# Who stores c and when x is asked for, in the first stage of a two-layer LoRA and FFN kernel

## The reference

```python
def _L0_cond_ref(x, adapter_mapping, W, b, lora_As, lora_Bs):   # x: (128 batches, 32 tokens, 512)
    base_out = einsum('bti,oi->bto', x, W) + b                   # W: 512 x 512
    A  = lora_As[adapter_mapping]                                # per batch: 512 x 16
    Bm = lora_Bs[adapter_mapping]                                # per batch: 16 x 512
    lora_h   = einsum('bti,bir->btr', x, A)
    lora_out = einsum('btr,bro->bto', lora_h, Bm)
    return base_out + lora_out * SCALING
x = x + _L0_ffn_ref(_L0_cond_ref(x, itok_B_0_23, ...), ...)      # silu(c Wg) * (c Wu) Wd, 512 -> 1376 -> 512
x = x + _L1_ffn_ref(_L1_cond_ref(x, itok_B_0_7, ...), ...)       # two layers with routers and experts
```

## Time and profile before

| what | value |
|---|---|
| median of 3 runs | 1004.67 us (1004.18 to 1007.02) |
| profiled execution, its own time | 1005.67 us |
| its span in the trace | 1003.9 us |
| TensorE busy | 979.7 us, 98% of the span, 4723 matmuls |
| VectorE / ScalarE / GpSimd busy | 591.7 / 464.6 / 255.2 us |
| chain that ended last | 81% TensorE, 9% SyncE's queue, 3% DMA, 3% VectorE |
| DMA | 230.15 MB, mean 229 GB/s |

### The profile page before, as it was taken

One profiled execution on the slowest core, in us unless ns is written; L12 is line 12 of the kernel. 1 busy time (PEld: TensorE's weight loads), 2 busy tenths in 40 slices (PEclk: granted clock), 3 DMA queues, 4 the chain that ended last, 5 costly groups with the idle time before them and its releaser, 6 DMA issues.

```text
span 1003.9 us, 14252 instructions
## 1 busy us (share of the span) xinstructions
PE 979.7 (98%) x4723; PEld 826.1 (82%) x4723; DVE 591.7 (59%) x969; ACT 464.6 (46%) x854; POOL 255.2 (25%) x244
## 2 busy tenths in 40 slices
PE   7998988999999999999999999999999999999998
PEld 6877877888888888888888888888888899898986
DVE  3665468676696343298333378443358588686862
ACT  3654555555472333474233366133357264445342
POOL 3332113455410431330161140063140280000000
PEclk9999999999999999999999999999999999999999
DMA  6888777667777886787986687797679650716132
GB/s 210 308 294 279 238 240 267 234 249 261 262 262 255 311 280 194 222 268 233 320 278 195 192 277 275 244 298 227 196 219 374 220 206 22 241 33 230 64 105 85
DMA packets 132772, 230.15 MB, mean 229 GB/s; under 512 B 30678, under 2 KB 30679, under 8 KB 131291
## 3 DMA queue, kind: packets, MB, share of 16 engines
q1 hardware_dynamic: 131184, 225.01, 67.0%
q0 software_dynamic: 1376, 4.22, 1.3%
q10 hardware_dynamic: 138, 0.01, 0.0%
HBM read 165.74 MB, written 63.44 MB: 228 GB/s over the span
## 4 chain that ended last, share of the span: by engine, by line
PE 81%; SPq 9%; DMA 3%; DVE 3%; issue 2%; ACT 1%; ACTq 0%; DVEq 0%
PE bank L1858 81%; SPq L559 4%; SPq L553 1%; DMA wring<-wd_scratch 1%; DVE xa_lo L1421 1%; SPq L759 1%; SPq L624 1%; PE bank L2011 1%; DMA slot_i<-in_slots 1%; DMA c<-c_scratch 1%; DMA a_raw<-in_a_cols 0%; SPq L558 0%; DMA x_raw<-in_x 0%; DVE b_lo L1436 0%; SPq L545 0%
## 5 line engine op out<-in xcount | busy, mean ns | idle before, releaser
L1858 PE MATMUL bank<-cop_hi,wring 128*128 128x512 f32 x1234 | 381.1, 390 | 1.3 <-issue 1.3
L1858 PEld LDWEIGHTS bank<-cop_hi,wring 128*128 128x128 f32 x1234 | 231.7, 188 | 49.9 <-issue 1.1
L1858 PE MATMUL bank<-cop_lo,wring 128*128 128x512 f32 x616 | 239.9, 389 | 0.0
L1858 PE MATMUL bank<-op_hi,wring 128*128 128x512 f32 x560 | 174.1, 390 | 0.1
L1508 DVE TENSOR_TENSOR v<-bank,p7s 128x512 f32<-128x512 f32 x44 | 30.4, 692 | 205.1 <-PE bank L1858 205.1
L1858 PEld LDWEIGHTS bank<-cop_lo,wring 128*128 128x128 f32 x616 | 115.7, 188 | 23.9
L1858 PEld LDWEIGHTS bank<-op_hi,wring 128*128 128x128 f32 x560 | 105.2, 188 | 22.4 <-DMA wring<-wd_scratch 0.5
L1858 PE MATMUL bank<-op_lo,wring 128*128 128x512 f32 x280 | 109.1, 390 | 0.0
L1107 ACT ACTIVATE s<-bank 128x512 f32<-128x512 f32 x44 | 26.4, 599 | 119.8 <-PE bank L1858 119.7
L1494 DVE TENSOR_TENSOR op_lo<-h,op_hi 128x512 fp32r<-128x512 f32 x100 | 72.9, 747 | 4.0 <-ACT op_hi L1064 3.8
L1064 ACT ACTIVATE op_hi<-h 128x512 fp32r<-128x512 f32 x100 | 62.7, 627 | 14.0 <-PE bank L1858 13.1
(11 more groups left out here) (225 smaller groups left out, 1922.8 us busy)
## 6 DMA issues: line engine op xcount, KB each, us to landing
wring<-wgu_scratch SPq DMA_DIRECT2D x231, 256.0 KB, 3.0
wring<-wd_scratch SPq DMA_DIRECT2D x140, 256.0 KB, 5.5
wgu_scratch<-wring SPq DMA_DIRECT2D x77, 256.0 KB, 3.5
c_scratch<-c_out SPq DMA_DIRECT2D x32, 256.0 KB, 6.0
c<-c_scratch SPq DMA_DIRECT2D x32, 256.0 KB, 3.2
xs_raw<-x_scratch SPq DMA_DIRECT2D x16, 512.0 KB, 6.0
out<-res SPq DMA_DIRECT2D x32, 256.0 KB, 2.1
x_raw<-in_x SPq DMA_DIRECT2D x7, 1024.0 KB, 9.3
```

Source lines behind the costliest of these rows:

```text
L1858: return e.matmul(out_ap, lhs, rhs, start=start, stop=stop, skip_group_check=True)
```

## The change

SyncE no longer stores c: GpSimd does, at the end of each tile's work, after its gathers of B and its weight sums. From tile 1 on, x comes in two DMAs of 512 KB instead of one of 1 MB; for x of tiles 3 to 7, one of them stands before each half of the gather of A, where the whole load stood before the first half. The load of x of tile 2 stays behind the gather of tile 1. The slot registers are 16 instead of 32 and are loaded before every gather. `slot_sb` gets a semaphore of its own, and SyncE waits for that alone. VectorE splits the first chunk of x and of W before it computes the rows of B.

```diff
-        return [[0], [1], [2, 3]] if t == 0 else [[0, 1, 2, 3]]
+        return [[0], [1], [2, 3]] if t == 0 else [[0, 1], [2, 3]]
...
-        slot_regs = [e.alloc_register(f"slot{n}") for n in range(2 * NG * GB)]
-        def gather_a(t):
-            n = NG * GB
-            if t % 2 == 0:
-                e.reg_load(slot_regs, slot_sb[0:1, t * n:(t + 2) * n])
-            for g in range(NG):
+        slot_regs = [e.alloc_register(f"slot{n}") for n in range(NG * GB)]
+        def load_slots(t):
+            e.reg_load(slot_regs, slot_sb[0:1, t * NG * GB:(t + 1) * NG * GB])
+        def gather_a(t, gs=range(NG)):
+            for g in gs:
...
-        e.wait_ge(slots_in, 2 * DMA)
+        e.wait_ge(slot_list_in, DMA)
+        load_slots(0)
         gather_a(0)
...
         for t in range(NT):
+            if t + 1 < NT:
+                load_slots(t + 1)
+            for g in range(NG):
+                if t + 2 < NT and t > 0:
+                    load_x(t + 2, x_parts(t + 2)[g])
+                if t + 1 < NT:
+                    gather_a(t + 1, (g,))
             if t == 0:
-                gather_a(t + 1)
                 load_down(1)
-            if t + 2 < NT:
-                for ks in x_parts(t + 2):
-                    load_x(t + 2, ks)
-            if 0 < t < NT - 1:
-                gather_a(t + 1)
+                for ks in x_parts(2):
+                    load_x(2, ks)
...
             for m in range(KC):
-                e.wait_ge(c_closed, nth(t, m))
-                e.dma_start(c_dram[t, m], c_out[m][:, :]).then_inc(c_stored[m], DMA)
...
+            for m in range(KC):                       # in pool_program, at the end of tile t
+                e.wait_ge(c_closed, nth(t, m))
+                e.dma_start(c_dram[t, m], c_out[m][:, :]).then_inc(c_stored[m], DMA)
...
-        e.wait_ge(slots_in, 2 * DMA)                  # in dve_program
+        split_x(0, (0,))
+        e.wait_ge(slots_in, DMA)
         linked(e.tensor_scalar(row_i[:, :], slot_i[:, :], float(R), r_f[:, 0:1], ALU.mult, ALU.add))
-        split_x(0)
+        split_x(0, range(1, KC))
```

More of the change, by code:

```diff
@@ L276, in build @@
     out_done = [sem(f"out_done{m}") for m in range(KC)]
-    w0_in = [sem(f"w0_in{k}") for k in range(KC)]
+    w0_in = [sem(f"w0_in{k}") for k in range(KC - 1)]
+    slot_list_in = sem("slot_list_in")
     a_in = [sem(f"a_in{g}") for g in range(NG)]
@@ L557, in gather_a @@
                 for b in range(GB):
-                    slot = e.snap(slot_regs[(t % 2) * n + g * GB + b], min_val=0, max_val=a_cols.shape[0] - 1)
+                    slot = e.snap(slot_regs[g * GB + b], min_val=0, max_val=a_cols.shape[0] - 1)
                     e.dma_start(a_raw[:, g, b, :], a_cols[bass.ds(slot, 1)].rearrange("s p c -> (s p) c")).then_inc(
@@ L1208, in turn_h @@
             e.activation(hi[:, :], bank[:, :], ACT.Copy).then_inc(hgt_hi_done, 1)
-        e.dma_start(slot_sb[0:1, :], slot_list).then_inc(slots_in, DMA)
+        e.dma_start(slot_sb[0:1, :], slot_list).then_inc(slot_list_in, DMA)
         e.dma_start(slot_i[:, :], slots.unsqueeze(1).to_broadcast([GB, R, n_batch // GB])).then_inc(slots_in, DMA)
```

## The result

The changed kernel takes 992.2 us (median of 4 runs, 991.1 to 994.51), the kernel before, timed beside it, 1005.56 us (4 runs, 1004.18 to 1007.02). The ratio is 0.987, 95% interval 0.9846 to 0.9894: 1.3% faster, where 988.7 us was forecast. The medians differ by 13.4 us. The profiled executions took 1005.67 and 991.1 us, which is 14.6 us less, as the one of the changed kernel is the fastest of its four; their spans are 1003.9 and 989.4 us.

A forecast was written before the change was run, and what follows sets the result against it. SyncE's queue, running behind, was taken to make TensorE wait before 160.93 us. Gains of 4.0 + 15.7, less 1.1 (c read back), 1.0 (ws) and 1.5 (late A or x), make 16.1 us: 988.7 us, range 982.5 to 997.5.

The forecast's parts named there:

- the likeliest case: Whole kernel: SyncE's queue runs behind and the change removes most of the waits, giving 988.7 us; chance 0.54.
- the early gather: Sign at the start: SyncE's first gather of A begins before 6.5 us, where it began at 10.13 us.
- s(7) at 143 to 145 us: Sign: tile 7's `lh_hi,b_hi` matmuls start (s(t) is that start in tile t) near 143 to 145 us, before 160.93.
- Start: Before tile 0's `lh_hi,b_hi` matmuls: earlier gather and x of tile 1 move their start from 27.77 to 23.5 us, gaining 4.3.
- Tile 1: Tile 1's `lh_hi,b_hi` matmuls start at 40.6 us instead of 44.56, so 4.0 of the start's 4.3 us stay.
- Tiles 2 and 3: Their 2.4 us of loss should go, as A lands with a margin of 6 us.
- Tile 4, tiles 5 and 6: Losses of 4.8 us (tile 4, wait for a_lo) and 0.1 us (tiles 5 and 6) go, clock included.
- Margins of SyncE: Tiles 2 to 7: A lands 6 us before it is wanted, 1.3 us with the dearest register load.
- Stores of c on GpSimd: Each tile: four stores of 1.2 us each, 4.8 us in all; nothing waits, VectorE is not slowed, cost 0.
- the rival that GpSimd becomes the bound: Every tile: stores of c above 3.1 us each fill GpSimd and the kernel gets slower, 1010.7 us at 3.9; chance 0.09.
- Tile 7: Of 8.4 us lost, c_out's 4.22 us wait goes less 1.0; lh_lo, behind c read back, is 1.1 late instead of 2.39.
- Halves of x, 16 registers: SyncE's queue: 16 registers load in 1.6 us instead of 2.07; half of x before each half of A lands in time.

The follow-up runs named there:

- n_wd_later: Changed kernel with the load of the second group of down weights moved from tile 0 to tile 1, behind the gather of A for tile 2: 992.07 us, 0.9874.
- n_c_first: Changed kernel with GpSimd's stores of c ahead of its down weight sums in tiles 0 to 5: 991.3 us, ratio 0.9885.
- n_best: Changed kernel with x whole, c stored ahead of the weight sums, and tile 7's second weight sums held until lh_lo is written: 990.73 us, ratio 0.9865.
- u_c_on_sync: Changed kernel with the stores of c back on SyncE, between the stores of dt: 1003.17 us, ratio 0.9978 to the kernel before.
- u_regs32: Changed kernel with 32 slot registers loaded before tiles 0, 2, 4 and 6: 992.02 us, ratio 0.9862 to the kernel before.
- n_sums_late: Changed kernel, but in tile 7 GpSimd holds its second four weight sums until lh_lo of tile 7 is written: 990.24 us, ratio 0.9867.
- n_gu_early: Changed kernel with the first gate and up weights loaded before the gather of A for tile 7 instead of behind it: 991.76 us, ratio 0.9869.

## Why the prediction was right, and where it was off

The forecast was 16.1 us, the profiled executions differ by 14.6 (the medians by 13.4), and the likeliest case is the one that came: SyncE's queue was what ran behind, and without c it keeps up from tile 3 on. Of the signs that the prediction names, the early gather and the FFN of 843 us came; s(7) at 143 to 145 us (146.46), no wait on a_lo (2.98 us in tile 2) and stores near 1.2 us (0.56) did not. Step by step:

- **Start** (4.3 us): the mechanism as told, 5.4 measured (27.77 to 22.33). The gather began at 5.28 instead of 5.5, the first register load took 1.17 instead of 1.6 us, and the gather ended at 13.9, as worked out. The surplus is in the landing of x: ScalarE took it up at 17.74 us, 3.8 us after its issue, where I carried over 4.86 from the earlier trace rows. Halving x is not the reason: with x whole s(0) is 22.60. What makes it land sooner stays open.
- **Tile 1** (4.0 stay): s(1) came 4.75 us sooner (44.56 to 39.81), 0.8 more than forecast.
- **Tiles 2 and 3** (2.4 us go, at a margin of 6 us): this step failed. They lost 2.4 us before and lose 3.5 now. Of the 4.75 us 3.8 are left at s(3). I took the issue of 8 gathers at 4.2 us, and a landing of 2.2 from the median of all; here the share is 1.05, the halves take 6.81 and 5.51 us to issue, and the second 5.5 to land. The margin went like this: the second half was issued by s(1) + 6.3 instead of + 1.0, and landed 3.3 us later than the 2.2 allowed, 8.6 us in all against a margin of 6; 2.98 us of waiting came of it. The prediction did have it: its average share of 0.93 "fits, but with little to spare", priced at 1.5 us. My reading is that an average hid the first three tiles, which, with two down weights and x sent ahead, ask for more than the engines give, and for which an earlier start of TensorE leaves less time. That waits were pushed from tile 2 to tile 3 but not out (n_wd_later, n_c_first, n_best) fits it. But I made no run with less traffic in all, and the share alone does not set the issue time: the next eight gathers, from 54.40 us on, took 4.01 us at a share of 1.01. So this cause is argued and not shown.
- **Tile 4, tiles 5 and 6** (4.8 and 0.1 us): 4.9 and 0.3. Right in size. The clock is 1.00 there, where it was 0.92.
- **Margins of SyncE.** For the changed kernel they held from tile 3 on. That they were a matter of waits was wrong, as u_c_on_sync shows: what counts is the sum of issues in a tile, 17.4 us (and more) with c and about 2 us less without.
- **Stores of c on GpSimd** (1.2 us each, 0.33 to 1.49): 0.56, and no wait. The nearest in kind, the gather of B, was a poor measure, as its issue stayed at 1.23. GpSimd's sums and these stores don't reach the bound of 3.1 us each by far; the rival that GpSimd becomes the bound is out. The bound itself was a little too high: GpSimd is busy for 34.9 us in the seven tiles of the earlier trace rows, 5.0 a tile and not 4.5, which makes 2.95 us. That nothing on VectorE is slowed holds for the stores, but I looked at the gathers alone and not at the sums.
- **Tile 7** (6.3 us of 8.4): 5.4. The wait on c_out is gone, also the 1.0 us that I left for it. `ws_scratch` was issued at s(5) + 7.5 and taken up at + 15.2, as forecast (+ 8 and + 15). c was read back on time: issued at s(6) + 6.2, in place of + 5.8, and c_t didn't wait for it. The 2.90 us are VectorE's, most of them from GpSimd's sums, and this the prediction doesn't have: it put lh_lo down to c read back, where the trace of the kernel before already shows the long splits. That the tile still came out within 0.9 us of the forecast is in part luck.
- **Halves of x, 16 registers**: I gave 16 registers part of the start and a part of SyncE's time. s(0) shows nothing of it (u_regs32). Loads of 16 take 0.97 to 3.35 us, as against 2.07 to 6.35, but twice as many; the total of either can't be told apart.

Sum: 3.8 (to s(3)) + 4.9 + 0.3 + 5.4 = 14.4 us against 16.1. Tiles 2 and 3 fell 2.6 us short and tile 7 0.9, of which the 1.5 us allowed for late A or x and 0.3 more in tiles 4 to 6 made up 1.8; the start's surplus of 1.1 us was given back by s(3).

## What to carry to other kernels

Add up what a queue issues in one period and hold it against the period: SyncE's queue with 17.4 us of issues in a tile of 16.68 was the bound, though no single wait in it looked fatal, and four stores a tile moved to another queue were worth 9 us alone and 11 us in the changed kernel. Take the DMA share stretch by stretch, at the stretch where loads are sent ahead: near 1.0 a landing time read elsewhere does not hold, and here another order only moved the wait. When a wait remains, read the engine named for operations that take longer than others of their shape, and look at what its neighbour does at that time.

## What the runs showed of the hardware

- VectorE's float32 operations on two tensors take longer beside GpSimd's: 128 x 256 in 0.95 us (some up to 1.48) instead of 0.41, 128 x 512 in up to 1.23 instead of 0.69, and the slow ones move with the sums when these are moved (n_sums_late, n_gu_early). Issuing a store from GpSimd is no such load: in n_sums_late, where no sum follows the stores at once, four stores run from 139.16 to 141.38 us, and the splits beside them take 0.41 us. (In the changed kernel one split beside the stores took 0.96 us, at 138.45; there the sums follow, and times on GpSimd are rough.) The changed kernel's 32 stores took 0.54 to 0.60 us each. The Trainium skill (SBUF — State Buffer, A bandwidth-pool intuition that's wrong (but worth ruling out)) gives 3100 ns for a DMA issued by GpSimd beside a copy on VectorE; no run here shows that for these operations.
- SyncE's issue of the same 8 gathers of 32 KB varies. In the changed kernel the two slowest, 6.81 and 5.51 us, fell on DMA shares of 1.00 and 1.05 (each over its own time); those issued from 70 to 113 us took 3.99 to 5.03 us at shares of 0.69 to 0.95. But eight took 4.01 us at 1.01, so the share is not all that sets it.
- What a wait of TensorE cost did not follow its length alone. Beyond 16.68 us, tile 2 lost 3.5 us at a wait of 2.98 (changed kernel, granted clock of the stretch 1.00), 4.9 at 2.99 (n_gu_early, 0.92, the same code up to there) and 6.9 at 3.95 (u_regs32, 0.86); tile 3 lost 3.9 at 2.21 (n_best, 0.92) and 6.5 at 3.07 (n_wd_later, 0.85). So executions that wait about the same differ by up to 3 us, as much as the halves of x or the sums could bring.
